# Turning the normalised tiles without TensorE: 32 by 32 squares on VectorE, then transfers between partition groups

## What is computed

```python
x = x + 0.5 * ffn(layernorm(x))
x = x + attention(layernorm(x))      # 32 query heads, 8 key heads of width 32, rotary, causal
x = x + 0.5 * ffn(layernorm(x))

def ffn(h):
    logits = h @ gate_w.T                        # 8 experts
    weights, selected = top_k(logits, 2); weights = softmax(weights)
    result = h @ base_w.T + base_b               # 1024 x 1024
    low = einsum('bsd,erd->ebsr', h, lora_A)     # rank 16 for each expert
    return result + 2.0 * einsum('ebsr,eor,bse->bso', low, lora_B, w_full)
```

## Time and profile before

| | before |
|---|---|
| median of 3 executions | 1513.42 us |
| lowest, highest | 1511.14, 1517.42 us |
| profiled execution, its own time | 1512.09 us |
| its span | 1510.3 us |
| granted TensorE clock, mean | 0.999 of 2.4 GHz |
| TensorE (PE) busy | 1483.6 us, 98% |
| VectorE (DVE) busy | 953.0 us, 63% |
| ScalarE (ACT) busy | 581.5 us, 39% |
| GpSimd (POOL) busy | 697.3 us, 46% |

### The profile page before, as it was taken

The page is one execution under the profiler, slowest core; times in us unless marked ns, Lnnn a source line. Parts: engine busy times, 40 slices in busy tenths (PEclk is TensorE's granted clock), DMA queues, the critical chain, the costliest instruction groups (busy, mean ns, idle before and its releaser), DMA issues. The chain is left out here.

```text
span 1510.3 us, 25951 instructions
## 1 busy us (share of the span) xinstructions
PE 1483.6 (98%) x9216; PEld 1187.3 (79%) x9216; DVE 953.0 (63%) x2726; ACT 581.5 (39%) x1058; POOL 697.3 (46%) x384
## 2 busy tenths in 40 slices
PE   7999999999999999999999999999999999999999
PEld 7999999888888875555555555555489999999988
DVE  6645455655563858888998888888465343433433
ACT  4333332221211126666666666666542122221210
POOL 1332322443334438999999999999503010100100
PEclk9999999999999999999999999999999999999999
DMA  6323232542416162543333444330262112121201
GB/s 240 129 100 115 99 128 101 177 141 87 140 70 161 69 166 61 113 96 79 79 79 79 108 106 99 78 79 23 64 238 77 49 56 71 43 83 42 83 15 42
DMA packets 118725, 146.01 MB, mean 97 GB/s; under 512 B 40896, under 2 KB 77120, under 8 KB 118336
## 3 DMA queue, kind: packets, MB, share of 16 engines
q1 hardware_dynamic: 90304, 121.37, 28.0%
q10 hardware_dynamic: 28304, 23.14, 4.7%
HBM read 95.72 MB, written 53.51 MB: 99 GB/s over the span
## 5 line engine op out<-in xcount | busy, mean ns | idle before, releaser
L1698 ACT ACTIVATE at_probs<-ps 128x512 f32<-128x512 f32 (+1 forms) x640 | 314.9, 561 | 163.7 <-PE ps L1607 157.8
L69 DVE CUSTOM_DVE_ANT_0 ps<-ps,at_score_mask 128x512 f32<-128x512 f32 (+1 forms) x480 | 270.3, 622 | 23.5 <-PE ps L1596 21.8
L349 POOL TENSOR_TENSOR f_x_ring<-f_x_ring,f_half_bias 128x1024 f32<-128x1024 f32 x32 | 78.1, 2444 | 309.3 <-DVE f_h L638 303.1
L1539 POOL TENSOR_TENSOR at_added<-at_added,at_probs 128x2048 f32<-128x2048 f32 (+1 forms) x60 | 210.5, 3509 | 2.7 <-ACT at_probs L1698 0.9
L1624 PE MATMUL ps<-at_probs,at_vs 128*32 128x512 f32 (+3 forms) x1536 | 150.2, 494 | 0.3 <-POOL at_probs L1518 0.3
L75 PE MATMUL f_ps<-f_wt_hi,f_hT_hi 128*128 128x400 f32 (+1 forms) x384 | 133.4, 347 | 3.2 <-DVE f_hT_lo L642 3.2
L75 PE MATMUL ps<-f_wt_hi,f_hT_hi 128*128 128x400 f32 (+1 forms) x384 | 131.4, 342 | 0.0
L77 PE MATMUL f_ps<-f_wt_hi,f_hT_lo 128*128 128x400 f32 (+1 forms) x384 | 130.8, 341 | 0.0
L76 PE MATMUL f_ps<-f_wt_lo,f_hT_hi 128*128 128x400 f32 (+1 forms) x384 | 130.6, 340 | 0.0
L76 PE MATMUL ps<-f_wt_lo,f_hT_hi 128*128 128x400 f32 (+1 forms) x384 | 130.2, 339 | 0.0
L77 PE MATMUL ps<-f_wt_hi,f_hT_lo 128*128 128x400 f32 (+1 forms) x384 | 130.0, 338 | 0.0
(11 more groups left out here) (206 smaller groups left out, 3591.1 us busy)
## 6 DMA issues: line engine op xcount, KB each, us to landing
f_x_ring<-in_L_attn_resid SPq DMA_DIRECT2D x16, 512.0 KB, 3.5
x<-f_x_ring SPq DMA_DIRECT2D x16, 512.0 KB, 2.6
early<-x SPq DMA_DIRECT2D x16, 512.0 KB, 3.4
scr_q_hi<-qkv_rope_hi ACTq DMA_DIRECT2D x32, 256.0 KB, 2.0
scr_q_lo<-qkv_rope_lo ACTq DMA_DIRECT2D x32, 256.0 KB, 2.3
scr_ctx<-at_ctxn SPq DMA_DIRECT2D x32, 256.0 KB, 2.4
shared<-scr_ctx SPq DMA_DIRECT2D x16, 512.0 KB, 4.5
f_x_ring<-x SPq DMA_DIRECT2D x16, 512.0 KB, 3.7
```

The costliest lines, as they stand in the source:

```text
L69: return dve.tensor_tensor_reduce(out=src[:, 0:keys], in0=src[:, 0:keys], in1=mask, scale=1.0, scalar=part_max[:, g, own] if c else -3.0e3 ...
L349: pool.tensor_tensor(x_ring[:, u, :], x_ring[:, u, :], half_bias[:], ALU.add).then_inc(bias_added, 1)
L1539: pool.tensor_tensor(added[:, heads, :], first, probs[:, (NU * n + u) % PROBS, heads, :], ALU.add).then_inc(added_done, 1)
L1698: act.activation(probs[:, (NU * n + u) % PROBS, g, cols], score_ps[x % BANKS][:, cols], ACT.Exp, scale=SCALE).then_inc(exp_done, 1)
```

## The change

The first three tiles of the first stage, the first four of `qkv_stage` and the first of the last stage are turned by TensorE as before. The other 13, 12 and 15 tiles, 40 in all, take another way:

- VectorE turns the normalised tile in squares of 32 by 32 (`to_blocks`, one instruction over 128 by 1024) into a buffer `blocks`. In the first two stages that is the fourth tile of `early`, in the last one a tile of its own.
- SP moves the squares between partition groups (`exchange`): 16 DMAs for a tile, one for each pair of a source and a destination group of 32 partitions. Each moves 32 partitions by 8 runs of 32 numbers (128 bytes), 32 KB. They land in `hT_lo` as float32.
- ScalarE makes `hT_hi` from there and VectorE overwrites `hT_lo` with the difference. Both now read SBUF in place of PSUM.
- There is one `blocks` buffer: `to_blocks` of the next tile waits until the exchange has landed (`landed`).
- The order of the steps moves. In the first stage VectorE and ScalarE normalise tile t+2 ahead of `low_lowT(t)` and `low_hT(t + 1)`. In the last one `to_blocks(t + 2)` stands behind `add_ffn(t)`. In `qkv_stage` `to_blocks` stands behind `normalize`, and `high_hT`, `low_hT` come one pair of groups later.
- In `ffn_stage` SP starts the exchange of tile t+2 once the first part of `lora(t)` is done. In the first stage it stands ahead of the store of x of tile t, in the last behind it.

The core of the diff:

```diff
+SQ = 32
+EXCHANGED = (P // SQ) ** 2 * 16
...
+def exchange(sp, blocks, landing, loaded):
+    for a in range(P // SQ):
+        for b in range(P // SQ):
+            src = blocks[a * SQ:(a + 1) * SQ, :].rearrange("i (c b j) -> i c b j", b=P // SQ, j=SQ)[:, :, b, :]
+            sp.dma_start(landing[b * SQ:(b + 1) * SQ, :, a * SQ:(a + 1) * SQ].bitcast(F32), src).then_inc(loaded, 16)
...
+    FROM = 3 if prep else 1
...
+            def turn(t, par):
+                sp.wait_ge(h_ready, t + 1)
+                if not (isinstance(t, int) and t < 2):
+                    sp.wait_ge(ffn_done, 3 * t - 4)
+                exchange(sp, blocks, hT_lo[:, par, :, :], h_turned)
+            if attn:
+                turn(1, 1)
...
+                if prep and more >= 2 and not by_tensor(t + 2):
+                    turn(t + 2, u % 2)
                 sp.wait_ge(ffn_added, 3 * t + 6)
                 own = x_stored if prep and isinstance(t, int) and t == NT - 1 else stored[u]
                 sp.dma_start(x_dst[bass.ds(t * P, P), :], x_ring[:, u, :]).then_inc(own, 16)
+                if attn and more >= 2:
+                    turn(t + 2, u % 2)
...
             def step(i, t, u, more):
-                if more >= 1:
-                    turn_h(t + 1)
+                if prep and isinstance(t, int) and t == 2:
+                    pe.wait_ge(ffn_added, 3 * t + 3)
                 base(t, u % 2, 0)
-                turn_low(t, more >= 1)
+                turn_low(t, False)
...
+                src = hT_ps if by_tensor(t) else hT_lo[:, par, :, :].bitcast(F32)
+                act.activation(hT_hi[:, par, :, :], src, ACT.Copy).then_inc(hT_hi_done, 1)
...
                 gap_exp(t)
+                if prep and more >= 2:
+                    deviation(t + 2)
                 act.wait_ge(ffn_done, 3 * t + 1)
+                high_lowT(t)
                 if more >= 1:
                     high_hT(t + 1, (u + 1) % 2)
-                high_lowT(t)
...
+            def to_blocks(t):
+                if not by_tensor(t - 1):
+                    dve.wait_ge(h_turned, landed(t - 1))
+                wait_apart(dve, ln_step, norm_steps(t, 5), passed)
+                dve.transpose(blocks, h[:]).then_inc(h_ready, 1)
...
                 routing(t, u % 2)
+                if prep and more >= 2:
+                    layer_norm(i, t + 2, u + 2)
+                low_lowT(t)
+                if prep and more >= 2:
+                    to_blocks(t + 2)
                 if more >= 1:
                     low_hT(t + 1, (u + 1) % 2)
-                low_lowT(t)
...
                 add_ffn(t, u)
+                if attn and more >= 2:
+                    to_blocks(t + 2)
...
+            def turn(t):                                   # qkv_stage, SP
+                sp.wait_ge(in_blocks, t - TC + 1)
+                if t >= NCH * TC:
+                    sp.wait_ge(v_done, (t // TC - 1) * TC + 1)
+                exchange(sp, blocks, tile_of(hT_lo, t), h_turned)
...
-                    if more and o % 2 == 1 and o // 2 < TC:
-                        turn_h(b, (ch + 1) * TC + o // 2)
...
-                    if more and o % 2 == 1 and o // 2 < TC:
-                        low_hT(b, (ch + 1) * TC + o // 2)
+                    if more and o % 2 == 1 and o > 1:
+                        low_hT(b, (ch + 1) * TC + o // 2 - 1)
```

More of the change, by code:

```diff
@@ L750, in _ @@
                 add_ffn(1, 1)
+                to_blocks(3)
             else:
@@ L759, in _ @@
                 layer_norm(0, 1, 1)
+                to_blocks(1)
                 for c in range(4, KC):
@@ L937, in _ @@
             for t in range(TC + 4, NT):
+                turn(t - 2)
                 load_x(t, t % 2)
+            for t in range(NT - 2, NT):
+                turn(t)
             sp.wait_ge(v_done, (B * NCH - 1) * TC + 1)
@@ L957, in _, with turn_h @@
             pe.sem_inc(v_done, 1)
-            def turn_h(b, t, first_tiles=False):
-                tile = b * (NCH * TC) + t
-                if not first_tiles:
-                    pe.wait_ge(h_ready, tile + 3)
-                    pe.wait_ge(hT_lo_done, tile + 1)
-                hT_ps = turned_ps[t if first_tiles else 0]
-                rows = early[:, t, :] if first_tiles else h
+            def turn_h(t):
                 for c in range(KC):
-                    last = pe.transpose(hT_ps[:, c, :], rows[:, c * P:(c + 1) * P], ident[:])
+                    last = pe.transpose(turned_ps[t][:, c, :], early[:, t, c * P:(c + 1) * P], ident[:])
                 last.then_inc(h_turned, 1)
             for t in range(TC):
-                turn_h(0, t, first_tiles=True)
+                turn_h(t)
             def by_pairs(outs):
```

69 lines of the change are left out of this document (48 added, 21 removed).

## The result

| | before | after |
|---|---|---|
| median | 1515.42 us (4 runs) | 1536.72 us (4 runs) |
| lowest, highest | 1511.14, 1518.78 | 1535.31, 1538.23 |
| ratio, 95% interval | | 1.0144, 1.0124 to 1.0164 |
| span of the profiled run | 1510.3 | 1533.8 |
| granted TensorE clock, mean | 0.999 | 0.989 |

What follows compares the result with a forecast made beforehand. TensorE, busy for 98% of the span, was taken as the bound. -34.8 + 1.3 + 1.5 + 1.4 = -30.6 us took the profiled 1512.09 to 1481.5; the median's 1.3 above it gave 1482.8 us, range 1475 to 1506.

Steps and rivals of the forecast that it cites:

- What is removed: TensorE, all three stages: 40 tiles of eight transposes at 0.87 us a tile, 34.8 us off its sequence.
- The exchange: SP's 16 DMAs: 0.51 us an issue (0.37 to 0.59), 8.2 together, last landing 2.0 after issue, 10.2 in all.
- SP in the first stage: 16 issues on top of 4.8 us make 13.0, which fits TensorE's 14.27 us pace until an issue costs 0.59.
- rival 3: SP's issue at 0.62 to 0.68 us; at 0.65, 12 us and 1495; chance 0.12 together with TensorE's time going unused.
- Tile 3: First stage, a tile without lead: TensorE waits about 1.3 us, once, for the exchange, `to_blocks(4)` and `low_hT(3)`.
- VectorE in `qkv_stage`: A pair of groups becomes 14.1 us; VectorE ends at 404.2, tied with TensorE's next chunk; 1.5 us for three chunks (0 to 6).
- The last stage's start: `to_blocks(1)` stands in VectorE's row of work, which is ahead of TensorE on the path: 1.4 us, once.
- covered by some 10 us: Last stage: a tile takes 26.0 us and the exchange starts behind `add_ffn`, with some 10 us of cover.
- Rival 2: VectorE becomes the bound: `to_blocks` costs 2.0 us, not 1.4; `qkv_stage` loses 7 us; 1490 us, chance 0.13.
- Rival 1: SP's issues cost more than any row shows: kernel slower from about 0.71 us, 1546 at 0.8; chance 0.13, page's rule included.
- DMAs that do not overlap: 16 landings of 2.0 us make SP's step 37 us, 294 us in the first stage, at least 1776 us; chance 0.02.
- The page's fit: The Trainium skill's 2.0 us plus bytes over 436 GB/s, giving 2.1 us for each 32 KB transfer of the exchange.

Runs made afterwards that it cites:

- the run with the other order: Only the first stage changed, 16 DMAs, with SP issuing the Wq load and weight copy while the tile's store lands, against the kernel before: 1522.41 us, ratio 1.0044.

## Why the prediction was wrong

**What is removed** was right. 0.87 us a tile is what TensorE gives back where it doesn't wait: 25.17 us for 26.04 in the last stage, 14.27 between exchanges in the run with the other order, 10.9 us in all of the first stage with 4 DMAs.

**The exchange** is the step that failed first. I took 0.51 us for an issue from the row with the same run length, with 0.59 as upper bound. It is 0.65 from issue to issue (10.43 us for 16) and 0.61 as a row, both above the upper bound. The bound came from the length of one row of 8 KB, and the distance to the next is longer than the row. The landing (2.0) was right. The exchange takes 11.8 us undisturbed, where the prediction had 10.2.

**SP in the first stage.** The threshold stood in the text: "until an issue costs 0.59 us". By rival 3's formula, 0.65 gives a pace of 15.2 us and 12 us. Measured are 15.3 to 16.6, with a mean of 15.8. That formula took SP's other work at 4.8 us, and it is 5.0 to 5.6, and an exchange is often interrupted (up to 11.3 us). I wrote the right rival and gave it 0.12 together with another, with a result of 1495, since it changed this stage alone. No rival had GpSimd's addition pushed into VectorE's routing by the late Wq load, which is what the waits for `low_s` are made of.

**Early loads** were not in the sum. Two waits for `add_ffn`, 5.7 us, stand behind them. The larger, 3.65 us, is SP's lateness again, against the same load before:

```profile
220.55 0.43 SPq L359 DMA_DIRECT2D early<-x  x1
225.19 1.29 DVE L741 BATCH_NORM_STATS2 f_early_stats<-early 128x6 f32<-128x512 f32 x2 [4.09 <-DMA early<-x]
```

```profile
203.79 0.42 SPq L323 DMA_DIRECT2D early<-x  x1
212.94 1.28 DVE L684 BATCH_NORM_STATS2 f_early_stats<-early 128x6 f32<-128x512 f32 x2
```

The load lands in 4.6 us, as before (4.8), but is issued 0.5 us before VectorE is free for it, where it had 9 us. Only the second (2.03 us) has a load that is itself slow, 6.0 us. With the other order of loads, where it is issued closer to the exchange, it takes up to 7.9.

**Tile 3** was to wait 1.3 us. It waits 1.85, in a kernel whose other waits soak up some of it, and 3.8 where they don't.

**VectorE in `qkv_stage`** was right to about 1 us: the last `low_hT` ends 65.8 us after the chunk's first reciprocal (348.22 to 412.81 plus 1.23), and the prediction had 64.7 (339.51 to 404.2). The consumer was wrong. I tied it to the start of TensorE's next chunk and called it a tie for 1.5 us. But ScalarE's `high_hT` of the same tile stands ahead of its first value copy, and TensorE needs that copy 7 us earlier: before, the copy was at 400.57 and the next chunk at 407.69. So the due date was missed by the 4 to 6 us that TensorE waits. I had checked what VectorE makes late for TensorE, and not what ScalarE, which waits for the same work, has queued behind it. To this comes the clock, half for 4 us and more behind two of the three waits, which no term had. The q stores, for which ScalarE waits in the same row of work, were in no term either.

**The last stage's start** had 1.4 us. It had the new instruction in it, and not GpSimd, which waits for the second `low_hT`. The end was "covered by some 10 us", which holds for every tile but the last.

**Rival 2** speaks of 7% slack that VectorE has in a pair. By the prediction's own numbers it is a deficit: 12.56 us on VectorE against 11.8 on TensorE.

**Rival 1**, slower through SP's issues, was the right sign at the wrong price: it needed 0.71 us alone. The kernel got slower at 0.65, since the other stages failed as well. DMAs that do not overlap would have made it at least 1776 us. The run has no trace of that: 16 are issued in 10.4 us, and the median one lands 2.0 us after its issue. The Trainium skill's rule for transfers under 64 KB (DMA: Bandwidth & Descriptors, Rules for kernel authors) says that one pays mostly overhead; here that overhead is the time of the issuing engine. The page's fit, which the prediction used for the 2.1 us of a transfer, was taken on DMAs that GpSimd issues; these are SP's, and the 2.0 us here are near it.

## What to carry to other kernels

A new queue of small transfers needs three dates and not one: when its issuing engine is free, when the last one lands, and when each engine that touches the result must be free for what stands behind it in its own order. The last is read from the program order of every consumer, not only of the one on the critical path. Where many small DMAs cost more than their data, count instructions: 4 plus 1 through DRAM, with twice the bytes, beat 16 within SBUF by 22 us here. And a wait that looks idle can hold an engine out of another's way, so look at what ran beside it before taking it out. The same holds for a load that comes later: it moved GpSimd's addition into VectorE's routing here. Last, read when a late load was issued before you call it slow.

The best version found leaves `qkv_stage` to TensorE and sends the squares of the other two stages through DRAM: 1496.0 us, ratio 0.9864 (0.9828 to 0.9901), or 1497.2 with no other change.

## What the runs showed of the hardware

- SP's issue of an SBUF to SBUF DMA with 128-byte runs is 0.61 us as a row and 0.65 from one to the next for 256 runs on 32 partitions, and 0.70 for 1024 runs on 128 partitions. A 512 KB load from DRAM in whole rows takes 0.34. The Trainium skill (Perfetto Trace Analysis, What "DMA-bound" means) names the issuing engine's sequencer as a bound of its own, filled with DMA slices that are not data movement. The trace agrees: SP is full for 10.4 us while each DMA's data is down 2.0 us after its issue.
- VectorE's block transpose of 128 by 1024 float32 takes 1.25 us (1.4 predicted), of 128 by 128 it takes 0.312. The Trainium skill (VectorE: DVE Perf Modes, The three transpose paths) gives 311 ns for that size in bf16; here it is the same in float32.
- VectorE's smallest instructions that read SBUF are held by GpSimd's 128x1024 work until it ends: 0.14 becomes 1.87 us (L709, a subtraction of two columns), 0.29 becomes 2.40 (L720, one tile and pointers), and 0.17 becomes 2.33 (L711, a cast of one tile, in nine tiles of the first stage). MAX8 from PSUM stays at 0.17. The Trainium skill (GPSIMD Engine Reference, Specifications) says that GpSimd's SBUF interfaces are shared with VectorE, with contention for instructions in a two-port performance mode or with two SBUF inputs. L709 agrees with the second case. L711 and L720 have one tile as input, so they would have to be in such a mode, which no run here shows.
- After a wait of 6.1 us TensorE's granted clock was 0.51 for the next 4 us, and this comes on top of the wait. The length of the wait does not decide it: after 3.49 us it was 1.00 in the change, and in the run with short exchange and value copies first it was 1.00 after 1.04 and 1.62 us, but behind the wait of 2.08 us at 461.87 it fell to 0.50:

```profile
464.00:466.00 2.00, 2.00 (x11) 2.00 (x10) 0.23 (x1) 1.44 (x2) 1.02 (x1) 0.50 0.42 158
```
